# Modulated convolutions on one core: first product in three parts, H's products split over PE's row halves, adds moved to GpSimd, first edges stored apart

## The chip, the cores and the metric

The kernel runs on one core of one Trainium2 chip. The metric is the device time of one launch in microseconds. Engines are named as in the profile: PE (matmuls), PEld (its weight loads), DVE (VectorE), ACT (ScalarE), POOL (GpSimd), SP (SyncE, which issues most DMAs). Everything is fp32.

## What is computed

32 samples, 64 channels, 1024 positions, passed through four style-modulated convolutions with 3 taps and added to the input:

```
TYPES = ('same', 'upsample', 'same', 'downsample')
s = style @ mw.T + mb
weight = SCALE * w * s[:, None, :, None]
demod = rsqrt(sum(weight * weight, axis=(2, 3)) + EPS)
weight = weight * demod[:, :, None, None]
# same: conv(x, weight) + b;   upsample: transposed conv, stride 2, + b, then a [1,3,3,1] blur
# downsample: [1,3,3,1] blur, then conv with stride 2, + b
x = x + layer3(layer2(layer1(layer0(x))))
```

## The kernel before

Samples go in 16 pairs, one sample on partitions 0 to 63 and one on 64 to 127. Layers 1 to 3 are linear between the edges, so for each pair the kernel composes their weights into seven 64x64 matrices, called `H`, and applies these to layer 0's output. Three positions at each end of a row ("edges") follow the four layers one by one; all samples' edges are computed once, spread over the first three pairs.

All matmuls of the main loop use a 64x64 quarter of PE's array. A matmul's quarter is given by the half of the rows that its inputs are in (partitions 0 to 63 or 64 to 127: "row half") and the half of the output partitions. Each matmul is two records in the trace, and each of them has a weight load.

The order of work is written by hand, with one queue of instructions for each engine and semaphores between them. An iteration p of PE's loop is: `layer0_odd(p+1)` into `p_lo`, `layer0_even(p+1)` into `p_le`, `product_2(p)` into `p_m2`, `compose_R(p+2)` into `p_lo`, `product_1(p)` into one half of `p_m13`, `compose_H(p+2)` into `p_le`, `product_3(p)` into the other half of `p_m13`. The products multiply blocks of `Hw` (H with sums of its blocks) with `u` (layer 0's outputs at odd places, and differences of even and odd ones) or with `uu` (differences of differences, from which `product_2` gets 256 columns out of three products of 128 columns).

- ACT in iteration p: copies `p_lo` to `u` (L599), scales layer 0's weights, copies part of `product_2` to `t_sb` (L611), copies R to `R_sb` in two instructions (L593), scales `A_sb`, copies H to `Hw` (L605). `compose_H` waits for `R_sb`.
- DVE in iteration p: `make_diffs(p+1)` (L729), `add_parts(p)` (L758), `make_uu(p+1)` (L750), in the first pairs an edge step, `sum_taps(p+2)` (L736 adds the second half of H; L740, L742, L743 add blocks of `Hw`), `finish(p)` (L787), `add_x(p)` (L794).
- SP in iteration p: `place_H(p+2)` (L252, L253: copies `Hw` across the partition halves; `product_2(p+2)` waits for it), `load(p+4)`, `store(p)`. `store(p)` waits for POOL to have put the edges into `ot` (L235), and these are only known in iteration 2.
- POOL: edge preparations (`xse` L205, `z_st` L214, `prod` L222, `y_st` L226), then the edges of each pair into `ot`.

Ahead of the loop ("prologue") stand the styles, the demodulation on DVE, R and H of pairs 0 and 1, and three small constants (`yc`, `zc`, `oc`) that PE and DVE hand to each other: PE's L477 needs `yc`, its L484 needs `zc` and ACT's `o_st`.

## Time and profile before

| | us |
|---|---|
| median of 3 runs (lowest, highest) | 181.14 (180.51, 181.2) |
| the profiled execution's own time | 181.34 |
| its span, first to last instruction | 179.2 |
| PE busy / DVE busy / ACT busy / POOL busy | 170.8 / 125.4 / 57.2 / 15.4 |

The span is read from the trace; what the profiled execution's own time has beyond it (2.1 us) lies around the instructions. "Busy" counts an engine with at least one instruction under way, so four quarters at work count once.

### The profile page before, as it was taken

What the parts mean: (1) busy time and instruction counts of PE and PEld (TensorE: products, weight loads), DVE (VectorE), ACT (ScalarE), POOL (GpSimd) and SP (SyncE); (2) the same over time, 40 slices, a digit from 0 to 9 for tenths busy, and PEclk for the clock granted to TensorE, in tenths of its full rate; (3) what the DMA queues carried; (4) which work ended last, traced back from release to release, by engine and by line L of the source; (5) the groups of instructions that cost most, each with busy time, mean ns of one, the idle gap of its engine ahead of it and who ended that gap; (6) DMA issues with size and microseconds to landing.
All of it is one profiled execution on the core that took longest, in us unless ns stands there. A gap on an engine that the chain in (4) does not pass through costs nothing.

```text
span 179.2 us, 7986 instructions
## 1 busy us (share of the span) xinstructions
PE 170.8 (95%) x3567; PEld 155.4 (87%) x3567; DVE 125.4 (70%) x265; ACT 57.2 (32%) x126; POOL 15.4 (9%) x47
## 2 busy tenths in 40 slices
PE   7899999999999799999999999999999999999990
PEld 5598969986677498999999999999999999998960
DVE  7659755896776946758494949494949394958793
ACT  3433554122142233324151514243332424222110
POOL 7002202800001300200000000000000000000000
PEclk9958999999999999999999999999999999999999
DMA  4960003033000986827274645456463637333322
GB/s 135 365 75 2 4 0 91 4 89 123 0 5 4 273 278 240 225 88 222 98 170 161 159 166 152 177 115 214 103 224 91 237 89 236 93 121 75 140 117 117
DMA packets 11778, 23.65 MB, mean 132 GB/s; under 512 B 5184, under 2 KB 5728, under 8 KB 11744
## 3 DMA queue, kind: packets, MB, share of 16 engines
q1 hardware_dynamic: 11680, 23.12, 42.8%
q8 instruction: 28, 0.46, 1.1%
q14 instruction: 6, 0.05, 0.1%
q10 hardware_dynamic: 64, 0.02, 0.1%
HBM read 8.85 MB, written 8.39 MB: 96 GB/s over the span
## 4 chain that ended last, share of the span: by engine, by line
PE 91%; DVE 3%; issue 2%; ACT 1%; DVEq 0%
PE p_m L415 26%; PE p_le L354 14%; PE p_lo L354 13%; PE p_le L398 12%; PE p_m L433 11%; PE p_lo L385 5%; PE p_le L304 2%; PE p_m L294 1%; PE p_le L402 1%; PE p_m L512 1%; PE p_m L505 1%; DVE r_sb L769 1%; PE p_m L285 1%; PE p_m L343 1%; PE p_m L495 1%
## 5 line engine op out<-in xcount | busy, mean ns | idle before, releaser
L415 PE MATMUL p_m<-u,Hw 64*64 64x256 f32 x896 | 61.0, 377 | 0.3 <-DVE z_sb L787 0.3
L415 PEld LDWEIGHTS p_m<-u,Hw 64*64 64x64 f32 x896 | 46.9, 132 | 2.6 <-issue 0.5
L354 PE MATMUL p_lo<-xin,w0s 64*64 64x259 f32 x384 | 31.0, 406 | 0.0
L736 DVE SCALAR_TENSOR_TENSOR Hw<-p_le,pvec,Hw 128x320 f32<-128x320 f32 x16 | 8.8, 551 | 31.0 <-ACT Hw L605 31.0
L354 PE MATMUL p_le<-xin,w0s 64*64 64x260 f32 x384 | 30.1, 407 | 0.2 <-DVE Hw L743 0.2
L398 PE MATMUL p_le<-R_sb,F_st 64*64 64x192 f32 x320 | 30.0, 324 | 0.0
L398 PEld LDWEIGHTS p_le<-R_sb,F_st 64*64 64x64 f32 x320 | 25.8, 133 | 1.1 <-issue 0.4
L354 PEld LDWEIGHTS p_lo<-xin,w0s 64*64 64x64 f32 x384 | 21.8, 137 | 2.4 <-issue 0.3
L354 PEld LDWEIGHTS p_le<-xin,w0s 64*64 64x64 f32 x384 | 20.7, 137 | 3.4 <-issue 1.1
L605 ACT ACTIVATE Hw<-p_le,pvec 128x448 f32<-128x448 f32 x16 | 10.2, 635 | 37.0 <-PE p_le L398 37.0
L787 DVE SCALAR_TENSOR_TENSOR z_sb<-p_m,pvec,s_sb 128x512 f32<-128x512 f32 (+1 forms) x30 | 21.0, 742 | 0.9 <-PE p_m L415 0.9
L729 DVE TENSOR_TENSOR u<-p_le,u 128x1036 f32<-128x1036 f32 x16 | 19.7, 1231 | 1.7 <-PE p_le L354 1.7
L599 ACT ACTIVATE u<-p_lo 128x518 f32<-128x518 f32 x16 | 9.7, 604 | 34.2 <-PE p_lo L354 34.2
L433 PE MATMUL p_m<-uu,Hw 64*64 64x128 f32 x512 | 20.0, 269 | 0.0
L402 PE MATMUL p_le<-R_sb,F_st 64*64 64x128 f32 x256 | 19.6, 278 | 0.0
L611 ACT ACTIVATE t_sb<-p_m,pvec 128x256 f32<-128x256 f32 x16 | 9.0, 565 | 32.9 <-PE p_m L433 32.9
L758 DVE SCALAR_TENSOR_TENSOR s_sb<-p_m,pvec,t_sb 128x256 f32<-128x256 f32 x32 | 14.1, 486 | 6.6 <-ACT t_sb L611 6.5
L794 DVE TENSOR_TENSOR ot<-xin,z_sb 128x1018 f32<-128x1018 f32 x15 | 18.3, 1222 | 0.5
L433 PEld LDWEIGHTS p_m<-uu,Hw 64*64 64x64 f32 x512 | 17.6, 132 | 0.0
L402 PEld LDWEIGHTS p_le<-R_sb,F_st 64*64 64x64 f32 x256 | 17.0, 132 | 0.0
L433 PE MATMUL p_m<-u,Hw 64*64 64x128 f32 x256 | 13.6, 278 | 1.1 <-issue 1.1
L433 PEld LDWEIGHTS p_m<-u,Hw 64*64 64x64 f32 x256 | 12.4, 131 | 2.3 <-issue 1.6
(122 smaller groups left out, 155.9 us busy)
## 6 DMA issues: line engine op xcount, KB each, us to landing
...
bn<-in_L_cond_mod_b_dram ACTq DMA_DIRECT2D x1, 1.0 KB
```

What stands on the lines that cost most here:

```text
L354: ins = pe.matmul(bank[h * C:(h + 1) * C, s, 0:n], w0s[p % 2][rows, k, :], xin[p % NX][rows, i0:i0 + 2 * n - 1:2], start=(k == 0), stop=(k ...
L398: ins = pe.matmul(p_H[s * C:(s + 1) * C, c * C:(c + NR) * C], F_st[0:C, c, :], R_sb[s][0:C, 0:NR].rearrange("p a c -> p (a c)"), start=(c ...
L402: pe.matmul(p_Ho[s * C:(s + 1) * C, (c + 1) * C:(c + NR) * C], F_st[C:P, c, :], R_sb[s][C:P, 0:NR - 1].rearrange("p a c -> p (a c)"), star ...
L415: ins = pe.matmul(bank(h)[s * C:(s + 1) * C], tap(p, h, s, blk), u[p % 2][h * C:(h + 1) * C, s, j, k:k + NM], start=(k == 0), stop=(k == l ...
L433: ins = pe.matmul(p_m2[s * C:(s + 1) * C, h, c * NQ:(c + 1) * NQ], tap(p, h, s, blk), moving(s, slice(h * C, (h + 1) * C), k), start=(k == 0),
L599: act.activation(u[p % 2][:, :, 1, 0:NO], p_lo[:, :, 0:NO], ACT.Copy).then_inc(uo_made, 1)
L605: act.activation(Hw[p % NW][:, 0, 0:NH], p_H[:, 0:NH * C].rearrange("p (a c) -> p a c", c=C), ACT.Copy, scale=pcol(W_A0, p)).then_inc(H_ev ...
L611: act.activation(t_sb[p % 2][:], p_m2[:, :, 0:NQ], ACT.Identity, scale=pcol(W_D3, p), bias=pcol(W_C, p))\
L729: dve.tensor_tensor(u[p % 2][:, :, 0:3:2, 0:NO], even, u[p % 2][:, :, 1, 0:NO].unsqueeze(2).to_broadcast([P, 2, 2, NO]), ALU.subtract)\
L758: dve.scalar_tensor_tensor(out=s_sb[p % 2][:, h].rearrange("p (j b) -> p b j", b=2), in0=p_m2[:, h, NQ:3 * NQ].rearrange("p (b j) -> p b j ...
L787: dve.scalar_tensor_tensor(out=to[:, n0 + 2 * m0:n0 + 2 * NM].rearrange("p (m a) -> p a m", a=2), in0=p_m13[:, h, :, m0:NM], scalar=pcol(W ...
L794: dve.tensor_tensor(ot[p % NO_T][:, EDGE:L - EDGE], xin[p % NX][:, EDGE + 1:L - EDGE + 1], z_sb[p % 2][:, EDGE:L - EDGE], ALU.add).then_in ...
```

## The change

`product_1` made 16 matmuls of 256 columns. It now makes 16 of 128 columns from `uu`, and 8 more of 128 columns, `product_1_mid`, into free columns 256 to 383 of `p_lo`, after `compose_H`. `make_uu` therefore makes twice as much, in two instructions, and DVE adds the middle part with `s_sb` into `e_sb` (`add_mid`, two instructions) before `sum_taps`. `finish` is four instructions of 254 or 256 columns in place of two of 506 or 512. `layer0_odd(p)` has a new wait, for `e_made` of pair p-2. `compose_H` had 10 matmuls of 192 columns on the first row half and 8 of 128 on the second; it has 6 of 128 and 4 of 192 on the first, and 8 of 128 and 6 of 64 on the second, for which POOL copies three blocks of `F_st` to the other half once (`F_dup`). `add_x` and the sums of blocks of `Hw` (`sum_blocks`, with one more instruction, for blocks 12 and 13) go from DVE to POOL, apart from those of pair 0 and a part of the last `add_x`. PE no longer waits for the sums of blocks, only for `H_added`. POOL's preparations come in another order, from the moment `e2` is made. Pairs 0 to 3 are stored without their edges as soon as `add_x` is done, and their edges later, in pairs 4 to 7, by two small DMAs each.

```diff
+        def sum_blocks(eng, p):
+            eng.wait_ge(H_added, p + 1)
+            w = Hw[p % NW]
+            eng.tensor_tensor(w[:, 0, 9:6:-1], w[:, 0, 2:7:2], w[:, 0, 1:6:2], ALU.add).then_inc(H_sums1, 1)
+            eng.tensor_tensor(w[:, 0, 12:14], w[:, 0, 6:1:-4], w[:, 0, 4::-4], ALU.add).then_inc(H_sums, 1)
+            eng.wait_ge(H_sums1, p + 1)
+            eng.tensor_tensor(w[:, 0, 10], w[:, 0, 7], w[:, 0, 8], ALU.add).then_inc(H_sums, 1)
+            eng.tensor_tensor(w[:, 0, 11], w[:, 0, 9], w[:, 0, 0], ALU.add).then_inc(H_sums, 1)
...
+            pool.wait_ge(made["e2"], 1)
...
+            pool.wait_ge(copied["F_st"], 1)
+            pool.tensor_copy(F_st[C:P, NF:], F_st[0:C, 0:3]).then_inc(made["F_dup"], 1)
...
+            def add_x(p, n0, n1):
+                pool.wait_ge(z_made, 4 * (p + 1))
+                wait(pool, stored[p % NO_T], 16 * (p // NO_T))
+                pool.tensor_tensor(ot[p % NO_T][:, n0:n1], xin[p % NX][:, n0 + 1:n1 + 1],
+                                   z_sb[p % 2][:, n0:n1], ALU.add).then_inc(out_made, 1)
...
+            sum_blocks(pool, 1)
+            for p in range(PAIRS):
+                if p > 0:
+                    add_x(p - 1, EDGE, L - EDGE)
+                if p + 2 < PAIRS:
+                    sum_blocks(pool, p + 2)
+                if p >= LATE:
+                    put_edges(p)
+            add_x(PAIRS - 1, EDGE, NX_L)
...
-                sp.wait_ge(edge_put, p + 1)
...
+                if p < LATE:
+                    sp.dma_start(rows[:, EDGE:L - EDGE], ot[p % NO_T][:, EDGE:L - EDGE]).then_inc(stored[p % NO_T], 16)
+                else:
+                    sp.wait_ge(edge_put, p - LATE + 1)
+                    sp.dma_start(rows, ot[p % NO_T][:]).then_inc(stored[p % NO_T], 16)
...
+                wait(pe, e_made, 2 * (p - 1))
                 layer0(p, p_lo, NO, 1, lo_done)
...
-                wait(pe, H_sums, 2 * min(p + 1, PAIRS))
+                wait(pe, H_added, min(p + 1, PAIRS))
                 layer0(p, p_le, NE, 0, le_done)
...
                 for c in range(NF):
                     for s in range(2):
...
+                        part(p_H, 0, s, c, 0, 2 if c < 3 else 3, c, start=(c == 0), stop=(c == NF - 1))
                         if c < NF - 1:
...
+                            part(p_Ho, 1, s, c, 0, 2, c + 1, start=(c == 0), stop=False)
+                if p == 0:
+                    pe.wait_ge(made["F_dup"], 1)
+                for c in range(3):
+                    for s in range(2):
+                        ins = part(p_Ho, 1, s, NF + c, 2, 1, c + 2, start=False, stop=(c == 2))
...
             def product_1(p):
...
+                wait(pe, z_made, 4 * p)
+                ww = uu[p % 2]
+                part(p, lambda h: p_m13[:, h, 0, 0:NQ], (6, 2), lambda rows, s, k: ww[rows, s, 0, 0, k:k + NQ])
+                part(p, lambda h: p_m13[:, h, 0, NQ:2 * NQ], (4, 0), lambda rows, s, k: ww[rows, s, 0, 1, k:k + NQ])\
+                    .then_inc(m1_done, 1)
...
-                product(p, lambda h: p_m13[:, h, 0, 0:NM], 0, (6, 4, 2, 0))
...
+                part(p, lambda h: p_lo[:, h, 2 * NQ:3 * NQ], (12, 13),
+                     lambda rows, s, k: w[rows, s, 0, 2 * k + 1:2 * k + 2 * NQ:2]).then_inc(mid_done, 1)
...
                     compose_H(p + 2)
+                product_1_mid(p)
                 product_3(p)
...
+            def add_mid(p):
+                dve.wait_ge(mid_done, p + 1)
+                dve.wait_ge(s_made, 2 * (p + 1))
...
-                dve.tensor_tensor(ot[p % NO_T][:, EDGE:L - EDGE], xin[p % NX][:, EDGE + 1:L - EDGE + 1],
-                                  z_sb[p % 2][:, EDGE:L - EDGE], ALU.add).then_inc(out_made, 1)
+                dve.tensor_tensor(ot[p % NO_T][:, NX_L:L - EDGE], xin[p % NX][:, NX_L + 1:L - EDGE + 1],
+                                  z_sb[p % 2][:, NX_L:L - EDGE], ALU.add).then_inc(last_made, 1)
...
+                add_mid(p)
                 if p + 2 < PAIRS:
                     sum_taps(p + 2)
                 finish(p)
```

On PE, from `product_1(3)` to the next pair's layer 0, the kernel before has:

```order
L415 MATMUL p_m<-u,Hw 64x256 x16
L398 MATMUL p_le<-R_sb,F_st 64x192
L402 MATMUL p_le<-R_sb,F_st 64x128
...
L398 MATMUL p_le<-R_sb,F_st 64x192
L402 MATMUL p_le<-R_sb,F_st 64x128
L398 MATMUL p_le<-R_sb,F_st 64x192 x2
L415 MATMUL p_m<-u,Hw 64x256 x12
L354 MATMUL p_lo<-xin,w0s 64x259 x12
```

The changed kernel has in the same place (its L484 is the helper of all products of 128 columns, L449 that of `compose_H`):

```order
L484 MATMUL p_m<-uu,Hw 64x128 x16
L449 MATMUL p_le<-R_sb,F_st 64x128 x12
L449 MATMUL p_le<-R_sb,F_st 64x192
L449 MATMUL p_le<-R_sb,F_st 64x128
L449 MATMUL p_le<-R_sb,F_st 64x192
L449 MATMUL p_le<-R_sb,F_st 64x128
L449 MATMUL p_le<-R_sb,F_st 64x192 x2
L449 MATMUL p_le<-R_sb,F_st 64x64 x6
L484 MATMUL p_lo<-u,Hw 64x128 x8
L474 MATMUL p_m<-u,Hw 64x256 x12
L404 MATMUL p_lo<-xin,w0s 64x259 x12
```

The first product is shorter and has a second piece behind `compose_H`, in `p_lo`, which the next `layer0_odd` writes again.

On DVE, iteration 3 of the loop before:

```order
L729 TENSOR_TENSOR u<-p_le,u 128x2x2x259
L758 SCALAR_TENSOR_TENSOR s_sb<-p_m,pvec,t_sb 128x2x128 x2
L750 TENSOR_TENSOR uu<-u 128x516
L736 SCALAR_TENSOR_TENSOR Hw<-p_le,pvec,Hw 128x320
L740 TENSOR_TENSOR Hw<-Hw 128x3x64
L742 TENSOR_TENSOR Hw<-Hw 128x64
L743 TENSOR_TENSOR Hw<-Hw 128x64
L787 SCALAR_TENSOR_TENSOR z_sb<-p_m,pvec,s_sb 128x2x256
L787 SCALAR_TENSOR_TENSOR z_sb<-p_m,pvec,s_sb 128x2x253
L794 TENSOR_TENSOR ot<-xin,z_sb 128x1018
```

And of the changed kernel (L806 is `make_diffs`, L832 `add_parts`, L824 `make_uu`, L843 `add_mid`, L813 `sum_taps`, L856 `finish`):

```order
L806 TENSOR_TENSOR u<-p_le,u 128x2x2x259
L832 SCALAR_TENSOR_TENSOR s_sb<-p_m,pvec,t_sb 128x256 x2
L824 TENSOR_TENSOR uu<-u 128x516 x2
L843 SCALAR_TENSOR_TENSOR e_sb<-p_lo,pvec,s_sb 128x256 x2
L813 SCALAR_TENSOR_TENSOR Hw<-p_le,pvec,Hw 128x320
L856 SCALAR_TENSOR_TENSOR z_sb<-p_m,pvec,e_sb 128x2x127
L856 SCALAR_TENSOR_TENSOR z_sb<-p_m,pvec,e_sb 128x2x128
L856 SCALAR_TENSOR_TENSOR z_sb<-p_m,pvec,s_sb 128x2x127
L856 SCALAR_TENSOR_TENSOR z_sb<-p_m,pvec,s_sb 128x2x128
```

Three additions of `Hw`'s blocks and `add_x` are gone from the queue; a second `make_uu` and two instructions of `add_mid` stand ahead of `sum_taps`.

On POOL, the preparations for the edges in the kernel before:

```order
L205 TENSOR_TENSOR xse<-xe,style 64x256 x2
L214 COPY z_st<-w2T 64x64 x6
L222 TENSOR_TENSOR prod<-wn,coef 64x256 x3
L226 TENSOR_TENSOR y_st<-y_st,prod 64x256 x3
L228 COPY y_st<-y_st 64x128
```

And in the changed kernel, up to its loop:

```order
L228 TENSOR_TENSOR prod<-wn,coef 64x256 x3
L232 TENSOR_TENSOR y_st<-y_st,prod 64x256 x3
L234 COPY y_st<-y_st 64x128
L237 COPY F_st<-F_st 64x192
L243 COPY z_st<-w2T 64x64 x6
L248 TENSOR_TENSOR xse<-xe,style 64x256 x2
L196 TENSOR_TENSOR Hw<-Hw 128x3x64
L197 TENSOR_TENSOR Hw<-Hw 128x128
L199 TENSOR_TENSOR Hw<-Hw 128x64
```

The six additions for `y_st` move from the loop (where they waited for `t_made`) to the front, and `xse` behind `z_st`.

## Rows read from the trace of the kernel before

**Rows 1.** The page, busy time of each engine.
```profile
PE 170.8 (95%) x3567; PEld 155.4 (87%) x3567; DVE 125.4 (70%) x265; ACT 57.2 (32%) x126; POOL 15.4 (9%) x47
```

**Rows 2.** The page, the chain that ended last, shares by engine.
```profile
PE 91%; DVE 3%; issue 2%; ACT 1%; DVEq 0%
```

**Rows 3.** Timeline of PE, one iteration: start us, length us, what.
```profile
90.25 0.28 PE L433 MATMUL p_m<-u,Hw 64*64 64x128 f32 x2
...
91.64 0.32 PE L385 MATMUL p_lo<-A_sb,V_st 64*64 64x128 f32 x1
...
92.27 0.38 PE L415 MATMUL p_m<-u,Hw 64*64 64x256 f32 x1
...
94.00 0.27 PE L402 MATMUL p_le<-R_sb,F_st 64*64 64x128 f32 x1
...
96.70 0.39 PE L354 MATMUL p_lo<-xin,w0s 64*64 64x259 f32 x1
...
99.56 0.28 PE L433 MATMUL p_m<-u,Hw 64*64 64x128 f32 x2
```

**Rows 4.** Timeline of PE and SP, first pairs.
```profile
27.84 0.68 PE L433 MATMUL p_m<-u,Hw 64*64 64x128 f32 x16
...
62.48 0.69 PE L433 MATMUL p_m<-u,Hw 64*64 64x128 f32 x16 [1.11 <-issue]
...
57.86 0.35 SPq L261 DMA_DIRECT2D out_dram<-ot  x1
58.30 0.54 SPq L252 DMA_DIRECT2D Hw<-Hw  x1
```

**Rows 5.** Timeline of ACT, the iteration of rows 3.
```profile
92.07 0.57 ACT L611 ACTIVATE t_sb<-p_m,pvec 128x256 f32<-128x256 f32 x1 [1.77 <-PE p_m L433]
92.64 0.73 ACT L593 ACTIVATE R_sb<-p_lo,vec 128x192 f32<-128x192 f32 x2
```

**Rows 6.** Timeline of DVE, the iteration of rows 3.
```profile
92.67 0.88 DVE L758 SCALAR_TENSOR_TENSOR s_sb<-p_m,pvec,t_sb 128x256 f32<-128x256 f32 x2 [0.30 <-ACT t_sb L611]
93.46 0.69 DVE L750 TENSOR_TENSOR uu<-u 128x516 f32<-128x516 f32 x1
96.62 0.55 DVE L736 SCALAR_TENSOR_TENSOR Hw<-p_le,pvec,Hw 128x320 f32<-128x320 f32 x1 [2.47 <-ACT Hw L605]
```

**Rows 7.** Timeline of POOL, its preparations.
```profile
13.66 1.21 POOL L205 TENSOR_TENSOR xse<-xe,style 64x256 f32<-64x256 f32 x2 [9.75 <-DMA xe<-in_x_dram]
...
30.15 2.46 POOL L222 TENSOR_TENSOR prod<-wn,coef 64x256 f32<-64x256 f32 x3 [10.01 <-ACT t_sb L611]
```

**Rows 8.** Timeline of DVE beside those of POOL.
```profile
11.92 0.37 DVE L679 TENSOR_TENSOR pvec<-style,dm 64x16 f32<-64x16 f32 x2
...
13.79 1.11 DVE L679 TENSOR_TENSOR pvec<-dm 64x16 f32<-64x16 f32 x2
...
17.16 0.34 DVE L805 RECIPROCAL dr<-dq 128x32 f32<-128x32 f32 x1
...
19.68 0.22 DVE L688 SCALAR_TENSOR_TENSOR yc<-vec,yc 128x32 f32<-128x32 f32 x1
...
30.10 0.88 DVE L758 SCALAR_TENSOR_TENSOR s_sb<-p_m,pvec,t_sb 128x256 f32<-128x256 f32 x2 [0.70 <-ACT t_sb L611]
30.89 1.16 DVE L750 TENSOR_TENSOR uu<-u 128x516 f32<-128x516 f32 x1
```

**Rows 9.** Timeline of PE, end of the prologue.
```profile
21.60 0.85 PE L477 MATMUL p_m<-yc,z_st 128*128 128x32 f32 x6
24.64 1.61 PE L354 MATMUL p_lo<-xin,w0s 64*64 64x259 f32 x24
```

**Rows 10.** Timeline of PE and DVE, the last two pairs.
```profile
164.90 0.62 PE L433 MATMUL p_m<-u,Hw 64*64 64x128 f32 x11
...
171.25 3.25 PE L415 MATMUL p_m<-u,Hw 64*64 64x256 f32 x56 [0.26 <-DVE z_sb L787]
...
174.68 1.40 DVE L787 SCALAR_TENSOR_TENSOR ot<-p_m,pvec,r_sb 128x512 f32<-128x512 f32 x2 [0.20 <-PE p_m L415]
```

More of the change, by code:

```diff
@@ L168, in modulated_conv_kernel @@
         s_made = sem("s_made")
-        r_made = sem("r_made")
+        e_made = sem("e_made")
         z_made = sem("z_made")
@@ L418, in product, with part @@
                 return ins
+            def part(p, bank, blocks, moving):
+                for k, blk in enumerate(blocks):
+                    for s in range(2):
+                        for h in range(2):
+                            ins = pe.matmul(bank(h)[s * C:(s + 1) * C], tap(p, h, s, blk),
+                                            moving(slice(h * C, (h + 1) * C), s, k), start=(k == 0),
+                                            stop=(k == len(blocks) - 1), skip_group_check=True)
+                return ins
             def product_2(p):
@@ L773, in finish @@
-            def finish(p):
+                    dve.scalar_tensor_tensor(out=e_sb[:, h].rearrange("p (b j) -> p b j", b=2),
+                                             in0=p_lo[:, h, 2 * NQ:3 * NQ].unsqueeze(1).to_broadcast([P, 2, NQ]),
+                                             scalar=pcol(W_D3, p),
+                                             in1=s_sb[p % 2][:, h].rearrange("p (b j) -> p b j", b=2),
+                                             op0=ALU.mult, op1=ALU.add).then_inc(e_made, 1)
@@ new lines, in finish, with parity @@
+            def finish(p):
+                def parity(a, from_, add):
+                    for h in range(2):
+                        n0, n = EDGE + h * BASE, BASE // 4 if h == 0 else NQ
+                        to = z_sb[p % 2][:, n0:n0 + 4 * n].rearrange("p (j b a) -> p b j a", b=2, a=2)
+                        dve.scalar_tensor_tensor(out=to[:, :, :, a], in0=from_(h)[:, :, 0:n], scalar=pcol(W_D3, p),
+                                                 in1=add[:, h].rearrange("p (b j) -> p b j", b=2)[:, :, 0:n],
+                                                 op0=ALU.mult, op1=ALU.add).then_inc(z_made, 1)
@@ L791, in add_x @@
-            def add_x(p):
-                dve.wait_ge(z_made, 2 * (p + 1))
+                    dve.wait_ge(m1_done, p + 1)
+                else:
+                    dve.wait_ge(m13_done, p + 1)
+                dve.wait_ge(e_made, 2 * (p + 1))
+                wait(dve, out_made, p - 1)
+                parity(0, lambda h: p_m13[:, h, 0].rearrange("p (b j) -> p b j", b=2), e_sb)
+                if last:
+                    dve.wait_ge(m13_done, p + 1)
+                odd = p_le[:, :, 0:NM] if last else p_m13[:, :, 1]
```

177 lines of the change are left out of this document (85 added, 92 removed).

## Prediction

> **What bounds the kernel now.** I read the page first: PE is busy for 170.8 of 179.2 us, DVE for 125.4 [rows 1]. Then the chain that ended last, 91% of it on PE [rows 2]. So DVE's and POOL's work counts only where PE waits for it, and I read one iteration on PE's timeline [rows 3]. It starts at 90.25 and the next at 99.56, 9.31 us. By first records: `product_2` 1.39 (to 91.64), `compose_R` 0.63, `product_1` 1.73 (to 94.00), `compose_H` and `product_3` together 2.70 (to 96.70), both halves of layer 0 2.86. Between pair 3's start (62.48) and pair 14's (164.90) lie eleven such, 102.4 us [rows 4, 10].
>
> How many columns does that stand for? `product_1` is four groups of four quarters, 256 columns each: 1.73/4 = 0.43 us a group, so 0.00169 us for a column in each quarter. `product_2` is six groups of 128: 0.232 each, against 0.216 for half of 0.43. So PE is bound by the columns of the fuller row half, and small groups cost some 0.015 us extra. In `compose_H` each quarter of the first row half has 5 x 192 = 960 columns, 1.62 us at that price, the second row half 4 x 128 = 512. With `product_3`'s three groups (1.30) the first row half would need 2.92; the 0.2 short of that comes back in layer 0, whose 1557 columns (3 x 519) beside it would need 2.63 and take 2.86. I therefore cost these stages as one.
>
> **The change on PE, per pair.** `product_1`'s 16 matmuls of 128 are four groups like `product_2`'s: 4 x 0.232 = 0.93. The middle part is two more, 0.46. Together 1.39 for 1.73: **-0.34**. `compose_H` falls from 960 to 3 x 128 + 2 x 192 = 768 columns on the first row half; the second gets 512 + 3 x 64 = 704, its short ones beside the last 192. By columns that is -0.32. The twelve records of 64 columns have no row of their own inside `compose_H`, so I bound them: nothing, or up to 0.15 us, since `compose_R`, which has 64s too, takes 0.63 for 320 columns (0.54 by price). I take 0.1: **-0.22**. Sum -0.56, to 8.75.
>
> **The wait that appears.** `compose_H` waits for `R_sb`. In the iteration of [rows 3] ACT made `t_sb` at 92.07 to 92.64 and both R at 92.64 to 93.37 [rows 5], 3.12 us after the iteration's start, while PE came at 94.00, so it had 0.6 to spare. ACT's row does not move: it hangs on `product_2`'s end. PE now comes 0.80 sooner, at 1.39 + 0.63 + 0.93 = 2.95, and waits until some 3.2: **+0.25**. Queued behind it on PE are the middle part, `product_3` and layer 0. Period 8.75 + 0.25 = **9.0**, -0.31 a pair, over eleven pairs **-3.4**.
>
> **DVE in that period.** `add_parts` ends at 3.2 (92.67 + 0.88) [rows 6]. Then `make_uu` twice: two of 0.69, overlapping a little, 1.3, to 4.5. The middle part ends on PE at 3.2 + 1.4 + 0.46 = 5.05, plus its last record's 0.27: 5.3. `add_mid` has two instructions of `add_parts`' size, 0.88, and ends at 6.3. `layer0_odd` now waits for it and would come after `product_3`, at 5.05 + 1.3 = 6.35. That is even, and I take 0. If `add_mid` is 0.1 later, each pair pays 0.1. Behind `add_mid` stand `sum_taps` (0.55, to 6.9) and `finish`, four instructions of 0.49 or less overlapping, to 8.6; the next `product_1` needs them at 9.0 + 2.0. DVE's sum is about 6.6 of 9.0: covered.
>
> **POOL.** `add_x` has 1018 elements. The nearest rows are two-input additions of 256 in 0.62 (1.21 for two) and 0.82 (2.46 for three, beside DVE's work) [rows 7]; four times that is 2.4 to 3.3. It starts at the end of `finish`, 0.4 before the next iteration, and ends at 2.0 to 2.9, before `make_uu` at 3.2. Then `sum_blocks`, about 1.5, from 6.9 to 8.4. Nothing waits: `Hw` is placed for two iterations later. The Trainium skill (GPSIMD Engine Reference, Performance versus the Vector engine) has 4497 ns for 2048 elements against DVE's 2293 and advises against such moves. An estimate from it is 2.2 us for `add_x`, near the rows; it would speak against the change only if POOL were on PE's path.
>
> **Prologue.** What POOL does to DVE stands in [rows 8]. Two tiny additions took 0.37 together at 11.92, but 1.11 at 13.79, beside `xse`: each ended with a POOL instruction. `make_uu` took 1.16 beside `prod` in place of 0.69. `add_parts`, with one input in PSUM, kept its 0.88. So a DVE instruction with two SBUF inputs waits for POOL's. The change starts `prod` when `e2` is made, at about 12.3: six instructions like `prod`'s three (2.46 [rows 7]), 4.9 us, to some 17. In it lie five such DVE instructions ahead of `make_diffs(0)`. Each may wait some 0.45: +2.2, less the 0.75 that `xse` costs there now, +1.4. A second `make_uu` adds 0.6, and `xse`, now beside the next demodulation (17.16 to 19.90 today), up to 0.7: `yc` comes at 22.6 instead of 19.90. PE would be ready for it at 21.60 - 0.3 (shorter H) and waits until 22.65. Behind come DVE's `sum_blocks(0)` with an extra instruction of 0.3, ACT's copy across, `o_st`; layer 0 of pair 1, at 24.64 now [rows 9], starts near 26.4. PE no longer waits there for the sums, -0.35. Sum **+1.4**, bounds -0.5 (POOL costs nothing) and +1.8. The rule of the Trainium skill (SBUF — State Buffer, "two separate sides") is the same: the shared ports are an exclusive lock for a whole instruction. The rows agree.
>
> **First pairs.** From 27.84 to 62.48 PE has 34.6 us. The 1.11 before pair 3 had no releaser by the trace; SP shows it: `place_H(3)` (58.30) stood behind `store(0)` (57.86), which waited for the edges [rows 4]. Stores of pairs 0 to 3 no longer do: **-1.1**. In these three iterations DVE's edge steps stand between `make_uu` and `add_mid`, so `layer0_odd` waits and the 0.3 a pair is mostly lost; I keep -0.5 in all. Bounds -2.5 and -0.8. The eight small DMAs lie beside idle queues: 0.
>
> **The end.** Today pair 14's start (164.90) is 9.8 before `finish(15)` (174.68) and 11.2 before its end [rows 10]. New: PE reaches `product_1(15)` 4.08 + 1.39 = 5.5 after, but `finish(14)` runs behind `add_parts`, two `make_uu` and `add_mid`: 3.2 + 1.3 + 0.9 + 1.7 = 7.1. PE waits 1.7 (today 0.26). Then 0.93 + 0.46 + 1.3 + 0.25: PE ends at 10.1. Second half of `finish` 0.9 after 10.6, to 11.55. Then the last add in two pieces, 634 elements on DVE (about 0.8) and 384 on POOL (about 0.9): 0.9 together, 1.7 if one holds up the other. That is 12.5 to 13.3 for 11.2: +1.3 to +2.1. Both have two SBUF inputs, so I take **+2.0**.
>
> **Sum.** +1.4 - 1.1 - 0.5 - 3.4 + 2.0 = -1.6, to a span of 177.6. The profiled execution, 181.34, would become 179.7. It is 0.2 above the runs' median of 181.14. Forecast **179.6**.
>
> **Rivals.**
> - *DVE isn't held up in the prologue*, its instructions slip between POOL's: -0.5 in place of +1.4 there, **177.7**; the end's two pieces side by side as well, 176.9. For it: POOL's six additions wait for one another and leave gaps. Against: [rows 8], twice. 0.2.
> - *`compose_H` doesn't wait*, because ACT has R ready 0.25 sooner: 11 x 0.25 = 2.7 less, 176.9. Nothing in ACT's queue moved. 0.05.
> - *Slower: `add_mid` stops `layer0_odd` in every pair.* Place: PE's wait for `e_made`. It has 0.05 us to spare. If DVE starts 0.1 later after PE than I think (0.20 before L787 [rows 10]) and reads the part of `p_lo`, broadcast, at 512-column speed (two in 1.1 to 1.4), the period is 9.3 and all of the steady gain is gone: -1.6 + 3.4 = +1.8, **183.0**. It decides against the change from about 0.15 a pair with the prologue as above. 0.15.
> - *The gains are real but the ends eat them*: prologue +1.8, first pairs -0.8, end +2.2, steady -3.0: 181.4, no change. 0.15.
> - The forecast itself, 178.3 to 180.6: 0.45.
>
> **Range and chances.** A difference of 0.5% (0.9 us) is about what a measurement of this kernel can tell. From the cases: faster than 180.2 0.61, slower than 182.0 0.18. The range reaches from the first rival to short of the slower one: 176.8 to 182.5.
>
> **What would show it.** PE's timeline of a middle pair: start to start 9.0, with about 0.25 idle before L449, 0 before L404. If L404 waits for L843, the slower rival holds. `product_1` 0.93. L477 near 22.6 and the two tiny additions before `make_diffs(0)` stretched. No wait before pair 3. L484 of pair 15 waiting about 1.7 for L856. The forecast is wrong if the period is under 8.8 or over 9.2, or if layer 0 of pair 1 starts before 25.

## The result and the profile after

The changed kernel takes **183.61 us** (median of 20 runs, 181.35 to 184.8), the kernel before 181.14 (median of 20, 180.42 to 182.52): ratio 1.0099 [1.0072, 1.0126], slower by 1%. The forecast was 179.6, faster. The profiled execution took 182.9 us with a span of 181.1, so it is 0.7 shorter than the median, and what is read from it is that much smaller. Here and below a time is the median of all executions, and a ratio, with its 95% interval, leaves out executions in the slow state, those more than 1.5% above the fastest of their kernel.

The page, busy time of each engine, the answer to [rows 1]:

```profile
PE 163.4 (90%) x4015; PEld 140.3 (77%) x4015; DVE 134.0 (74%) x285; ACT 57.0 (31%) x126; POOL 73.5 (41%) x120
```

PE is busy for 7.4 us less while the span is 1.9 us longer, so PE stands still somewhere. PE's timeline for a middle pair, the answer to [rows 3] (here a row is a whole group of matmuls):

```profile
128.03 0.66 PE L484 MATMUL p_m<-u,Hw 64*64 64x128 f32 x16
...
129.37 0.75 PE L436 MATMUL p_lo<-A_sb,V_st 64*64 64x128 f32 x24
129.93 1.07 PE L484 MATMUL p_m<-uu,Hw 64*64 64x128 f32 x32
131.18 1.53 PE L449 MATMUL p_le<-R_sb,F_st 64*64 64x128 f32 x48 [0.18 <-issue]
132.46 0.71 PE L484 MATMUL p_lo<-u,Hw 64*64 64x128 f32 x16
132.92 1.54 PE L474 MATMUL p_m<-u,Hw 64*64 64x256 f32 x24
134.26 1.60 PE L404 MATMUL p_lo<-xin,w0s 64*64 64x259 f32 x24
...
137.03 0.67 PE L484 MATMUL p_m<-u,Hw 64*64 64x128 f32 x16
```

128.03 to 137.03 is 9.00 us, the period of the forecast, with its small wait ahead of L449 (`compose_H`, for `R_sb`) and none at L404. The loss is in pairs that don't look like this. Call the time from one start of `layer0_odd` to the next an interval. From pair 4 to pair 15 there are eleven; they are 9.0 to 9.1 us, but for two: 11.13 (77.04 to 88.17) and 9.96 (97.18 to 107.14). PE's timeline in these two, and the weight loads at the first:

```profile
78.43 1.07 PE L404 MATMUL p_le<-xin,w0s 64*64 64x260 f32 x10
80.92 0.91 PE L404 MATMUL p_le<-xin,w0s 64*64 64x260 f32 x11 [1.42 <-issue]
...
103.11 1.20 PE L449 MATMUL p_le<-R_sb,F_st 64*64 64x128 f32 x32 [0.18 <-issue]
105.00 0.54 PE L449 MATMUL p_le<-R_sb,F_st 64*64 64x192 f32 x14 [0.68 <-issue]
...
80.93 0.42 PEld L404 LDWEIGHTS p_le<-xin,w0s 64*64 64x64 f32 x10 [1.90 <-issue]
```

PE stops in the middle of a group whose inputs it is already using, and the trace names no releaser. Such a stop is called a hole below. For its place, an iteration p is counted from the start of `product_2(p)`: the first hole is in iteration 4, in `layer0_even(6)`, the second in iteration 7, in `compose_H(9)`. The intervals lose more (2.1 and 0.95) than PE's idle shows (1.42 and 0.68), since the ends of matmuls are modelled.

Last, the two ends of the kernel: PE's timeline, the answer to [rows 9, 10], and DVE's and POOL's last rows:

```profile
22.35 0.83 PE L553 MATMUL p_m<-yc,z_st 128*128 128x32 f32 x6 [0.71 <-issue]
25.40 0.54 PE L560 MATMUL p_m<-zc,o_st 128*64 128x32 f32 x12 [0.77 <-ACT o_st L719]
25.88 1.61 PE L404 MATMUL p_lo<-xin,w0s 64*64 64x259 f32 x24
...
164.16 0.67 PE L484 MATMUL p_m<-u,Hw 64*64 64x128 f32 x16
...
171.52 1.11 PE L484 MATMUL p_m<-uu,Hw 64*64 64x128 f32 x32 [1.83 <-DVE z_sb L856]
...
176.27 0.82 DVE L877 TENSOR_TENSOR ot<-xin,z_sb 128x634 f32<-128x634 f32 x1
...
176.32 1.63 POOL L255 TENSOR_TENSOR ot<-xin,z_sb 128x384 f32<-128x384 f32 x1 [2.28 <-DVE z_sb L856]
```

By the forecast's own parts (`product_2` of pairs 0, 3 and 14 starts at 28.69, 61.81 and 164.16 in the changed kernel):

| part | before | forecast | after | off by |
|---|---|---|---|---|
| to pair 0 | 27.84 | 29.24 | 28.69 | -0.55 |
| pairs 0 to 3 | 34.64 | 33.04 | 33.12 | +0.1 |
| pairs 3 to 14 | 102.42 | 99.0 | 102.35 | +3.3 |
| pair 14 to the end | 14.3 | 16.3 | 16.9 | +0.6 |
| span | 179.2 | 177.6 | 181.1 | +3.5 |

### The profile page after: what moved, and what is told of

Read it like the earlier page. It is cut to its first block and busy times, and to the rows that moved or that the text cites. A ratio compares the mean times of both kernels' runs of the same rounds, so it can differ in the third digit from the quotient of the medians.

```text
span 181.1 us, 9008 instructions
## 1 busy us (share of the span) xinstructions
PE 163.4 (90%) x4015; PEld 140.3 (77%) x4015; DVE 134.0 (74%) x285; ACT 57.0 (31%) x126; POOL 73.5 (41%) x120
## 5 line engine op out<-in xcount | busy, mean ns | idle before, releaser
L255 POOL TENSOR_TENSOR ot<-xin,z_sb 128x1018 f32<-128x1018 f32 (+1 forms) x16 | 37.2, 2324 | 13.6 <-DVE z_sb L856 13.6
L484 PE MATMUL p_m<-uu,Hw 64*64 64x128 f32 x1024 | 35.3, 269 | 1.8 <-DVE z_sb L856 1.8
L484 PEld LDWEIGHTS p_m<-uu,Hw 64*64 64x64 f32 x1024 | 30.8, 132 | 2.1 <-DVE z_sb L856 2.1
L404 PE MATMUL p_le<-xin,w0s 64*64 64x260 f32 x384 | 27.5, 404 | 1.4 <-issue 1.4
L806 DVE TENSOR_TENSOR u<-p_le,u 128x1036 f32<-128x1036 f32 x16 | 19.8, 1235 | 11.9 <-PE p_le L404 11.9
L449 PE MATMUL p_le<-R_sb,F_st 64*64 64x128 f32 (+2 forms) x768 | 25.1, 269 | 2.7 <-issue 2.5
L404 PE MATMUL p_lo<-xin,w0s 64*64 64x259 f32 x384 | 27.2, 409 | 0.1
L449 PEld LDWEIGHTS p_le<-R_sb,F_st 64*64 64x64 f32 x768 | 21.6, 133 | 5.9 <-issue 5.7
L404 PEld LDWEIGHTS p_le<-xin,w0s 64*64 64x64 f32 x384 | 18.9, 137 | 6.5 <-issue 1.9
L843 DVE SCALAR_TENSOR_TENSOR e_sb<-p_lo,pvec,s_sb 128x256 f32<-128x256 f32 x32 | 14.0, 479 | 12.4 <-PE p_lo L484 12.4
L474 PE MATMUL p_m<-u,Hw 64*64 64x256 f32 x360 | 23.1, 375 | 0.0
L832 DVE SCALAR_TENSOR_TENSOR s_sb<-p_m,pvec,t_sb 128x256 f32<-128x256 f32 x32 | 14.0, 479 | 11.0 <-ACT t_sb L688 11.0
L404 PEld LDWEIGHTS p_lo<-xin,w0s 64*64 64x64 f32 x384 | 16.5, 137 | 6.7 <-issue 3.5
L824 DVE TENSOR_TENSOR uu<-u 128x516 f32<-128x516 f32 x32 | 20.7, 689 | 0.1
L856 DVE SCALAR_TENSOR_TENSOR z_sb<-p_m,pvec,e_sb 128x254 f32<-128x254 f32 (+1 forms) x32 | 18.7, 665 | 0.2
L474 PEld LDWEIGHTS p_m<-u,Hw 64*64 64x64 f32 x360 | 17.4, 132 | 0.5
L856 DVE SCALAR_TENSOR_TENSOR z_sb<-p_m,pvec,s_sb 128x254 f32<-128x254 f32 (+1 forms) x30 | 17.1, 652 | 0.0
```

Of the source, the lines that this page charges most:

```text
L255: pool.tensor_tensor(ot[p % NO_T][:, n0:n1], xin[p % NX][:, n0 + 1:n1 + 1], z_sb[p % 2][:, n0:n1], ALU.add).then_inc(out_made, 1)
L404: ins = pe.matmul(bank[h * C:(h + 1) * C, s, 0:n], w0s[p % 2][rows, k, :], xin[p % NX][rows, i0:i0 + 2 * n - 1:2], start=(k == 0), stop=(k ...
L449: return pe.matmul(bank[s * C:(s + 1) * C, to * C:(to + n) * C], F_st[rows, f, :], R_sb[s][rows, a:a + n].rearrange("p a c -> p (a c)"), s ...
L474: ins = pe.matmul(bank(h)[s * C:(s + 1) * C], tap(p, h, s, blk), u[p % 2][h * C:(h + 1) * C, s, j, k:k + NM], start=(k == 0), stop=(k == l ...
L484: ins = pe.matmul(bank(h)[s * C:(s + 1) * C], tap(p, h, s, blk), moving(slice(h * C, (h + 1) * C), s, k), start=(k == 0), stop=(k == len(b ...
L806: dve.tensor_tensor(u[p % 2][:, :, 0:3:2, 0:NO], even, u[p % 2][:, :, 1, 0:NO].unsqueeze(2).to_broadcast([P, 2, 2, NO]), ALU.subtract)\
```

## What the holes are

The page's list of DMA queues has one of kind "instruction", with 28 packets before and 32 after:

```profile
q8 instruction: 32, 0.52, 1.2%
```

0.52 MB in 32 packets is 16 KB each. Each f32 matmul is four instructions of PE, two loads and two passes (`compose_H`'s 24 matmuls show as x48, with x48 loads). Counted so, PE's program has 7,289 instructions before (1,787 matmuls and 141 others, nearly all waits) and 8,185 after (2,011 and 141), 28.5 and 32.0 times 256. So a packet is taken to be a block of 256 of them. A steady iteration has 432 instructions before and 488 after: a block lasts 9.31 x 256/432 = 5.5 us before and 9.0 x 256/488 = **4.7 us** after, on average. With the program numbered from 0, the holes stand at instruction 3280 = 13 x 256 - 48 and 4560 = 18 x 256 - 48. Places of the form 256k - 48 are called edges. Why 48 short of the full block no run shows, and the number depends on the count (the prologue's seven transposes, counted as four instructions each, show one load and one pass); that all holes share it does not.

The DMA view of the changed kernel has no packet of this queue from 74.0 to 78.4, where the load and the store of a pair fill the engines, and one behind them. The whole list of queues for 74 to 78.4, then for 78.4 to 79.5:

```profile
q1 hardware_dynamic: 280, 1.02, 74.4%
...
q8 instruction: 1, 0.02, 5.4%
q1 hardware_dynamic: 2, 0.00, 1.0%
```

5.4% of 16 engines over 1.1 us is 0.95 us, which ends at some 79.5, and PE goes on at 80.92. Where the DMA engines are little used, the packet mostly starts 0.4 to 1.5 us behind PE's passing of the edge before. Here that edge (12 x 256 - 48) was passed at 73.4. **Theory F**: PE has one block ahead and no more. The next is asked for at an edge; its transfer queues behind load and store; it must be there at the next edge, 4.7 us later on average. By these rows it needs some 0.8 to be asked for, 0.95 to move and 1.4 to be used. As an estimate, that leaves some 1.5 us for a queue, and load and store with H's transfers make up to 4.

The profiles of all the kernels below bear this out. Each has one packet for each edge of PE's program (28 before, 32 after, 35 in run 2, 30 in run 6). PE never passed an edge sooner than 1.2 us after the end of the packet that was asked for at the edge before. At the 37 edges where its weight loads stood still for more than 0.25 us, it went on 1.2 to 1.6 us after that end. In the kernel before, the closest case is 1.9 us: there the packets come in time.

The Trainium skill (Runtime: NRT & Kernel Launch, Instruction fetch mechanics) has the blocks of 16 KiB as 256 instructions, with which the counts agree, and calls the cost of crossing one "mostly hidden". Here it is 2.1 us for one crossing: the measurement decides. It also gives PE a store of 2048 instructions. The holes at one edge end behind the packet asked for at the edge before, so no run here shows more than one block ahead.

## Experiments

Each comparison is with the kernel before, run on the same chip.

**1. Stores cut short** (the changed kernel).

```
+                elif p < PAIRS - 1:
+                    sp.wait_ge(edge_put, p - LATE + 1)
+                    sp.dma_start(rows[:, 0:64], ot[p % NO_T][:, 0:64]).then_inc(...)
```

> The changed kernel with the stores of pairs 4 to 14 cut to their first 64 columns (the rest of those rows isn't written). Nothing that PE waits for changes. Theory F (PE's own instructions arrive late: they come by DMA in 16 KB blocks, and the block's transfer waits behind loads and stores): the two holes inside a stage, 1.42 and 0.68 us in the changed kernel's profile, are gone, every middle pair takes 9.0 us, the span falls by about 3 us to 178.0, the time to about 180. Theory D (the holes are a wait for data or for a buffer): holes and span stay, 181 us. What stays under both: prologue +0.85 and end +2.6 against the kernel before.

The kernel leaves most of these rows of the output unwritten. 181.89 us, 1.0047 [1.0019, 1.0075], where 180 was expected. The second hole went and every interval from 88 us on is 9.0 to 9.1. The first stayed, 1.41 at 80.81. It follows the store of pair 3, which this run left whole. So the next run cuts that too.

> Every store of pairs 0 to 14 writes the first 64 columns only (for pairs 0 to 3 columns EDGE to 64); the rest of those rows of the output is left unwritten, the last pair's is whole. In the run with only the stores of pairs 4 to 14 cut, TensorE's hole of 1.41 us at 80.8 stayed and the later one went. Theory F (TensorE waits for its own code, whose transfer stands behind the load and the store): with store 3 short too, the hole at 80.8 goes or falls under 0.3 us, all intervals of layer0_odd from pair 5 on are 9.0 to 9.1, span 178.2 to 178.8. Rival A (an engine's result is late there and the stores have nothing to do with it): the hole stays at 1.4 us, span 180.0. Rival B (the load alone holds the code up): the hole shrinks to 0.7 to 1.2 us, span 179.3 to 179.8.

180.89 us, 0.9943 [0.9903, 0.9982]. All eleven intervals from pair 4 to 15 are 8.99 to 9.03; no hole. The span, 179.3, missed the expected range, because this execution's first `layer0_odd` came at 10.64 (9.89 in the changed kernel's) and the prologue was 1.6 longer by pair 1 (27.44 for 25.88). Without that it is 177.7. Rivals A and B fall: the hole needs the store. That leaves open whether it needs its bytes or its place in the queue; run 10 tells.

**2. The kernel before with more instructions**: `product_1` and `product_3` in halves of 128 columns, 28 matmuls more for a pair, the same columns.

```
+                for q in (0, NQ):
                     for k, blk in enumerate(blocks):
```

> The kernel before with products 1 and 3 in halves of 128 columns: the same columns, data and DMAs, but 28 more matmuls a pair, each four instructions. Theory F: an instruction block of 256 lasts 4.5 us of work in place of 5.5, less than in the changed kernel (4.7), so holes without a releaser appear in the middle of stages, 3 us or more in all; with 0.2 us a pair for small groups (14 of 0.232 for 7 of 0.43) the span is 179.2 + 3.2 + 3 = 185.5 or more. Theory D: no such holes, only the small groups, 182.4.

191.08 us, 1.053 [1.0482, 1.0578]. An iteration has 544 instructions and its clean interval is 9.4, so a block lasts 4.4 us. The kernel that had no hole in its steady pairs now has four over 1 us, at 68.57, 119.71, 130.24 and 141.31, with intervals of 10.65 to 12.35, and 35 packets for 9,081 instructions. All four stand within one instruction of an edge. Nothing of the change is in it but the number of instructions.

**3. GpSimd's sums for `y_st` behind `sum_blocks(1)`** (the prologue's term).

```
             sum_blocks(pool, 1)
...
+            for k in range(K):
+                pool.tensor_tensor(prod[:, k], ...)
...
```

> The changed kernel with POOL's six additions for y_st moved from the moment e2 is made to behind sum_blocks of pair 1. If POOL's instructions hold up DVE's two-input ones in the prologue, the tiny additions before make_diffs(0) are back to about 0.2 us each, yc comes 1.5 us sooner and product_2(0) starts at 27.3 in place of 28.69; the first pairs may give 0.3 back, where make_uu(1) meets the additions. The time is 1 us lower than the changed kernel's if the holes stay as they are. If POOL does not matter, product_2(0) stays at 28.7.

182.08 us, 1.0044 [1.0016, 1.0073]. DVE's small instructions are short again (0.37 for the 0.92 that the changed kernel's `pvec` row shows at 14.72, below), but then `make_diffs(0)` waits for PE:

```profile
14.13 0.37 DVE L757 TENSOR_TENSOR pvec<-dm 64x16 f32<-64x16 f32 x2
15.80 1.24 DVE L807 TENSOR_TENSOR u<-p_le,u 128x1036 f32<-128x1036 f32 x1 [1.03 <-PE p_le L405]
```

So `product_2(0)` starts at 27.82, 0.9 sooner and not 1.4: layer 0 of pair 1 starts at 25.00 in place of 25.88, while the first interval grew by 0.36 (10.43 for 10.07). The holes stayed (1.15 at 80.11, 0.44 at 104.01).

**4. The load behind the store and behind `e_made`.**

```
+                store(p)
                 if p + 4 < PAIRS:
+                    sp.wait_ge(e_made, 2 * (p + 2))
                     load(p + 4)
-                store(p)
```

> The changed kernel with SP's queue in another order: store(p) first, and load(p+4) waits for e_made of pair p+1, about 4 us later, so that a load and a store no longer run together. Theory F: PE's instruction blocks wait behind one transfer of 0.5 MB (1.7 us) at most in place of two (4 us), the holes shrink to under 0.5 us in all, span 178.0 to 178.6. Theory D: no change, or worse if the load comes too late (it has 4 us to spare).

183.3 us, 1.0108 [1.0065, 1.015]: no gain. The two holes went and others came: 0.47 at 74.20, 0.97 at 137.26, 0.41 at 147.36. The largest stands at instruction 6352 = 25 x 256 - 48, an edge too; its packet came at 134.9, behind the load issued at 131.56. Where the DMA engines are busy decides which edge is hit.

**5. Useless waits to hold the edges in place.**

```
             def compose_H(p):
+                for _ in range(48 if p > 5 else 240 if p == 5 else 0):
+                    pe.wait_ge(ident_made, 1)
```

(two such waits make one instruction; 240 is 512 in the second run)

> Nothing of the computation changes. TensorE's program gets useless waits (on a semaphore that has long been set) ahead of compose_H: 96 + 24 instructions once, in iteration 3, and 24 in each iteration after it, so that an iteration from there on is 512 instructions, exactly two blocks of 256, and the edges of the blocks stand at one place of every iteration: 85 instructions behind the start of product_2 (1.2 us after it) and in product_1_mid (4.6 us). Theory F: the code's transfer is asked for some 0.8 us behind an edge, the first falls ahead of the load and the store, the second behind them but in time, so from pair 5 on TensorE has no hole over 0.3 us, however regular or not the intervals were before; each interval is 9.0 plus what 24 waits cost over the present wait there (0 to 0.6 us), all equal within 0.1. Rival A (the holes of 1.42 at 80.9 and 0.68 at 105.0 come from an engine that is late in those pairs): a hole of 0.5 to 1.5 us stays within one pair of either place.

> As the run with 96 + 24 waits in iteration 3, but 232 + 24 there, so that the two edges of blocks in each iteration stand 204 instructions behind the start of product_2 (2.9 us, at the end of product_1) and 460 behind it (7.5 us, in layer0_even), which is how they stood in the iteration of the hole at 80.9. The same number of instructions in each iteration as the other one. Theory F: the code asked for at 3.7 us waits behind the load and the store to 7.0 or later and TensorE stands 1 to 2 us at the start of layer0_even or behind it, in most iterations from 4 to 10, as long as there are loads: span 5 to 12 us over the other padded run beyond the 136 more waits (at most 4 us) in iteration 3. Rival A: no difference in the intervals of pairs 5 to 15 between the two padded runs.

218.03 us, 1.2048 [1.2006, 1.209], and 236.43, 1.3057 [1.2996, 1.3118]. Neither test decides anything, because of its own cost. An already satisfied wait of PE takes 0.115 us: 136 more instructions of waits in iteration 3 lengthen its interval from 22.93 to 38.59. PE's timeline in a middle iteration of the first:

```profile
111.59 1.07 PE L486 MATMUL p_m<-uu,Hw 64*64 64x128 f32 x32
114.63 1.53 PE L451 MATMUL p_le<-R_sb,F_st 64*64 64x128 f32 x48 [1.97 <-issue]
```

The 24 waits stop PE for 2 us in each iteration. Intervals from iteration 4 on are 10.8 to 11.0, every second or third one 12.4 to 13.0, in both runs, and no hole at `layer0_even` came in the second. A block then lasts 5.4 us or more, nearly the 5.5 of the kernel before, so theory F would have no hole either; the runs don't tell it from rival A. The long interval looked at, 117.71 to 130.09 of the first run, has a stretch at a granted clock of 0.50 behind the stop (busy of PE, PEld, DVE, ACT and POOL with counts, then granted clock, DMA share and GB/s):

```profile
128.00:130.00 2.00, 2.00 (x24) 1.92 (x20) 1.30 (x3) 0.00 (x0) 0.62 (x2) 0.50 0.00 0
```

**6. The old `compose_H` in the changed kernel** (22 lines back to the kernel before's).

```
-                        part(p_H, 0, s, c, 0, 2 if c < 3 else 3, c, ...)
+                        ins = pe.matmul(p_H[s * C:(s + 1) * C, c * C:(c + NR) * C], F_st[0:C, c, :], ...)
```

> The changed kernel with compose_H as it was: 22 matmuls with all of H's products in the order of before, the row halves uneven. The prediction's term was -0.22 us an iteration for the new compose_H, with R_sb's wait of 0.25 us beside it. With the old one compose_H takes 0.22 us more, and what it waits for R_sb is as before. So clean intervals of layer0_odd should be 9.22 to 9.25 if the term is right, and 9.0 if it is worth nothing. By theory F an iteration is then 480 instructions or less, not 488, and a block of code lasts 4.9 us: holes of TensorE move to other pairs or shrink, at 256k-48 instructions wherever they are; sum of holes over 0.3 us from 60 us on 0 to 2.5 us, median 182 to 185.

186.62 us, the median of four from 184.02 to 188.13; the ratio, 1.0207 [1.0147, 1.0268], rests on the two shorter ones, 184.02 and 185.82, whose mean is inside the expected range. The profile is of the longest, so its holes may be larger than usual. Its clean intervals are 9.33, above the expected range, so the new `compose_H` is worth 0.33 of them, not 0.22. Holes stand at instructions 2000, 4048 and, within two matmuls, 7120 (8, 16 and 28 x 256 - 48): 1.70 at 58.96, 0.96 at 102.30, 0.35 at 164.22. The old `compose_H` has 18 matmuls and not the 22 expected, so an iteration has 464 instructions and a block lasts 5.1 us; that did not save this order, since a hole comes where an edge meets busy DMA engines.

**7. PE's program shifted by 188 instructions.**

```
-            for _ in range(4):
-                pe.matmul(p_le[:, 1, 0:256], pe_warm[:, 0:P], pe_warm[:], start=True, stop=True)
+            for _ in range(51):
+                pe.matmul(p_le[0:C, 1, 0:8], pe_warm[0:C, 0:C], pe_warm[0:C, 0:8], start=True, stop=True)
```

> TensorE's four warm-up matmuls of 128x256 at the start (16 instructions, 3.8 us) are replaced by 51 small ones (204 instructions); nothing else changes, so every later instruction of TensorE stands 188 places further along its program, and the edges of the blocks of 256 move by 188 against the work. In the changed kernel the holes stood where an edge fell 204/460 and 276 instructions behind the start of a product_2, in iterations 4 and 7. Here such edges fall: 276 in iteration 4, 460 in iteration 12, where the DMA engines have no load left. Theory F: the hole of 1.4 us at layer0_even of iteration 4 is gone; one of 0.3 to 1.0 us stands in compose_H of iteration 4 or of 3; none from iteration 6 to 14; so the sum of late intervals falls from 3.1 to under 1.2 us and the median from 183.6 to 181.2 to 182.4. Rival A (a late engine): both holes stay in their pairs, median 183 to 184.5.

192.05 us, 1.0592 [1.0521, 1.0662]. The small matmuls took 11.05 us in place of 3.78, so the whole kernel starts 8.0 later; from there on the intervals are what was asked for. The hole of 1.42 at iteration 4's `layer0_even` is gone. Iteration 4 has a stop inside its `compose_H` instead, as expected, in the interval ahead (9.85), and those from pair 6 to 12 are 9.0 to 9.1. One part of the expectation is wrong. No hole was to come from iteration 6 to 14, since the edge in `layer0_even` of iteration 12 finds no load; that edge costs nothing indeed, but the one in `layer0_even(13)`, at the end of iteration 11, still meets the last load. It is the largest stop of all. PE's timeline, and the windows around it (columns as under run 5):

```profile
149.18 1.61 PE L404 MATMUL p_lo<-xin,w0s 64*64 64x259 f32 x24
152.78 2.71 PE L404 MATMUL p_le<-xin,w0s 64*64 64x260 f32 x24 [1.99 <-issue]
155.15 1.20 PE L484 MATMUL p_m<-u,Hw 64*64 64x128 f32 x16
...
151.00:153.00 2.00, 0.22 (x4) 0.20 (x7) 0.58 (x2) 0.79 (x2) 1.61 (x3) 1.00 0.41 82
153.00:155.00 2.00, 2.00 (x24) 1.72 (x20) 0.00 (x0) 0.00 (x0) 1.01 (x1) 0.51 0.53 155
```

Instruction 6864 = 27 x 256 - 48. The load and store ahead of it had been issued at 144.92 and 145.36, the packet came at 150.4. Behind the hole the granted clock was 0.51, the level of 1.2 GHz, and `layer0_even` took 2.71 for 1.59: the interval is 12.83, 3.8 over. So the same program with the same work has its largest hole seven iterations later when its instructions stand 188 further on. That is not a late engine.

**8. The ends.** Three edits: the order of run 3; `product_1` of the last pair into `p_lo`, waiting for `e_made`; the last add wholly on DVE. Alone, and with run 7's shift:

```
-                wait(pe, z_made, 4 * p)
+                last = p == PAIRS - 1
+                wait(pe, e_made if last else z_made, 2 * p if last else 4 * p)
...
-            add_x(PAIRS - 1, EDGE, NX_L)
```

> Three edits of the changed kernel at its ends: GpSimd's sums for y_st come behind sum_blocks(1), as in the run that gave 182.08 alone; product_1 of the last pair goes to p_lo and waits for e_made, not for the z_made of the pair before; VectorE does the whole last add. The forecast put the end at +2.0 and it was +2.6. If those 2.6 are product_1's wait of 1.83 us for z_sb and GpSimd's piece of 1.63 us, the two edits take 1.3 to 2.0 off (span from layer0_odd of pair 15 to the end 18.1 to 18.7 where it was 19.7) and with the order on GpSimd the median is 180.2 to 181.4. If the end is set by something else (VectorE's own chain), the end stays within 0.5 of 19.7 and the median at 181.6 to 182.6. Holes of TensorE stay at 256k-48 instructions.

> The three edits of the ends and the 51 small warm-up matmuls together. If the code's edges and the ends are separate costs, the gains add: holes from pair 5 on sum to under 1.2 us, end as in the run of the three edits, median 178.2 to 180.0, faster than before by 0.6 to 1.6%. If theory F is wrong, the median is that of the run of the three edits within 0.4.

The first: 180.62 us, 0.9944 [0.9911, 0.9978]. This is as expected: from `layer0_odd` of pair 15 to the end it takes 18.6 in place of 19.7. The wait of 1.83 for `z_sb` is gone and the last add is one row of DVE:

```profile
174.01 1.22 DVE L881 TENSOR_TENSOR ot<-xin,z_sb 128x1018 f32<-128x1018 f32 x1
```

The second, expected at 178.2 to 180.0: 188.64 us, 1.0431 [1.0371, 1.049]; as in run 7, the start pays 7.2 us, intervals lose 0.5 to 1.9 in three other places, and nothing is gained by shifting.

**9. The second evacuation of R by DVE.**

```
-                for s in range(2):
+                for s in range(2 if p < 2 else 1):
...
+                if p + 2 < PAIRS:
+                    evac_R1(p + 2)
```

> The second evacuation of R of each pair goes from ScalarE to VectorE, behind make_diffs, so that compose_H need not wait for it. The forecast put this wait at 0.25 us of each iteration. If it is so and nothing replaces it, clean intervals of layer0_odd fall from 9.00 to 8.75 to 8.85. If VectorE's longer queue delays the sums of z or the evacuation of H, they stay at 9.0 or rise. By theory F a block then lasts less than 4.6 us, the slack of the code's transfer is smaller and the holes of TensorE grow in number or size: late intervals sum to 3 to 6 us and the median is 182 to 185 in spite of the shorter clean interval.

181.64 us, 1.0001 [0.9971, 1.0032]. Clean intervals are 8.70 and `compose_H` has no wait, so the wait for `R_sb` was worth 0.30, not 0.25. Over eleven pairs that is 3.3 us, of which the times show 2.0 (183.61 to 181.64): the first three intervals grew by 0.8, and holes make intervals of 10.59, 9.95 and 9.35, together 3.8 over, where the changed kernel lost 3.1. A block lasts 4.6 us.

**10. The store later, nothing else.**

```
                 if p + 4 < PAIRS:
                     load(p + 4)
+                if p >= 3:
+                    sp.wait_ge(H_done, min(p + 4, PAIRS))
                 store(p)
```

> The changed kernel with one wait more: SyncE issues the store of a pair from 3 on behind compose_H of the running iteration, some 2 us later than now, so that the load (2 us of the DMA engines) and the store (2 us) no longer form one burst. All bytes are moved. Theory F: the code's transfer that stood behind both at 74.0 to 78.4 now gets in behind the load alone; TensorE's hole of 1.42 us at layer0_even of iteration 4 shrinks to 0 to 0.5 us, and the loss of that interval from 2.1 to under 1; the one in iteration 7 (asked for behind H's transfers, not the store) may stay; median 181.0 to 182.8. Rival B (the load alone holds the code up): the hole stays within 0.3 of 1.42, median 183 to 184. Rival C (the late store now stands ahead of H's placement, which is issued 6 us after the start of product_2, and product_2 waits): every interval grows by 0.3 to 1 us, median 186 or more.

**179.66 us, 0.9903 [0.988, 0.9925].** All bytes are moved, all instructions are there, and no hole is left: of the eleven intervals from pair 4 to 15 ten are 9.00 to 9.02 and the last 9.11. PE's timeline at the place of the first hole, SyncE's queue ahead of it, and the instruction queue for 75.3 to 76.7:

```profile
76.97 1.60 PE L406 MATMUL p_lo<-xin,w0s 64*64 64x259 f32 x24
78.36 1.59 PE L406 MATMUL p_le<-xin,w0s 64*64 64x260 f32 x24
...
72.89 0.33 SPq L283 DMA_DIRECT2D xin<-in_x_dram  x1
75.55 0.35 SPq L299 DMA_DIRECT2D out_dram<-ot  x1
...
q8 instruction: 1, 0.02, 4.5%
```

The load is issued at 72.89, the store only at 75.55, and the packet, at 75.6, goes in the gap between them: 3.0 us sooner than in the changed kernel. The gain was larger than expected (181.0 to 182.8), since the second hole went too: 3.9 us between the medians and 3.2 between the two profiled executions (182.9 and 179.7), where the two long intervals had lost 3.1.

**11. The same line in the kernel before.**

> The kernel before with the same late store (from pair 3 on the store waits for compose_H of the running iteration). Its steady intervals are 9.30 to 9.32 us with no hole, a block of code lasts 5.5 us there. Theory F: the late store gives back only what the changed kernel lost, so nothing is to be had here: intervals 9.30 to 9.32, median within 0.5 of 181.4. Rival D (the late store is an improvement of its own, whatever the code): median 179 to 180.5, as it took 3.9 us off the changed kernel. Rival C (it delays H's placement): intervals over 9.4, median over 182.

181.57 us, 0.9989 [0.9968, 1.001]: nothing. The line gives back what the change had lost and has no gain of its own.

**12. Together.**

> The three edits of the ends (180.62 alone) with the late store. If the late store takes the hole at layer0_even of iteration 4 (loss 1.58 in that run) and the rest stays, the median is 179.0 to 180.2; if it does nothing, 180.4 to 181.

> The three edits of the ends with VectorE doing the second evacuation of R. Clean intervals were 8.70 with it against 9.01, and eleven of them are 3.4 us; but first pairs grew by 0.5 to 0.8 us and the holes were as large as in the changed kernel. So the median should be 180.62 less 1.0 to 2.4: 178.2 to 179.6. If the shorter interval only makes larger holes, as the forecast's bare sum would not see, it stays above 180.

> All of it: ends, R by VectorE, late store. If the store's place is worth 0.5 to 1.6 us as theory F says, the median is that less than the run without it, 177.0 to 179.0; with a block of code lasting 4.5 us the slack is small, so one or two holes of 0.5 to 1 us remain.

Ends and late store 177.96, 0.981 [0.9789, 0.983]; ends and R by DVE 178.7, 0.9897 [0.9821, 0.9974]; all three **174.88**, 0.9643 [0.961, 0.9676]. The first and the last are under their expected ranges: the late store was to be worth 0.5 to 1.6 in the last and is worth 3.8. Without it intervals of 10.60, 10.17 and 9.40 stand among those of 8.70, with it only one, 9.07, with no hole. It is the fastest kernel of this study, 3.6% below the kernel before.

## Why the prediction was wrong

**The step that failed** is "Period 8.75 + 0.25 = 9.0, -0.31 a pair, over eleven pairs -3.4". The period is right to 0.01 us. What is wrong is to take it eleven times: pairs 3 to 14 gained 0.1 in place of 3.4. Of the 3.3 missing, 3.1 were lost in two intervals in which PE waited for its own program (runs 1, 2, 7, 10, 11); with the store later, all eleven came out at 9.0 to 9.1. The sum counted the columns of the new matmuls and never their instructions, which went from 432 to 488 an iteration, so it put a wait for them at nothing without a reason. The rival that came nearest to the time (183.0) had another mechanism, `add_mid` stopping `layer0_odd`, and that doesn't occur: a likeness of numbers. DVE's row of `add_mid` in the middle pair ends at 134.10, and L404 starts at 134.26 without a wait:

```profile
133.22 0.88 DVE L843 SCALAR_TENSOR_TENSOR e_sb<-p_lo,pvec,s_sb 128x256 f32<-128x256 f32 x2 [0.91 <-PE p_lo L484]
```

**`compose_H` and its wait**: -0.33 in place of -0.22 (run 6) and a wait of 0.30 in place of 0.25 (run 9). Together they would leave the period 0.06 shorter than forecast; by difference, `product_1` with its middle part gives -0.28 for -0.34, which makes that up.

**Prologue**: the mechanism held, +0.85 for +1.4. DVE's instructions beside POOL's `prod` and `y_st` are stretched, as the forecast had it:

```profile
13.42 0.60 DVE L765 SCALAR_TENSOR_TENSOR da<-da,dr 128x64 f32<-128x64 f32 x1
14.06 0.62 DVE L765 SCALAR_TENSOR_TENSOR dm<-da,dr 128x64 f32<-128x64 f32 x1
14.72 0.92 DVE L756 TENSOR_TENSOR pvec<-dm 64x16 f32<-64x16 f32 x2
15.67 0.60 DVE L760 TENSOR_SCALAR vec<-dm,biases 128x32 f32<-128x32 f32 x1
```

These five instructions took 1.06 us in run 3, where POOL is idle beside them, and 2.74 here: 1.7 more, where the forecast had 2.2. POOL's six instructions took 4.5 us for the 4.9 allowed and the rest of `yc`'s chain was less held up. The rival with no hold-up falls.

**First pairs**: 33.12 for 33.04; the wait of 1.11 before pair 3 is gone, as forecast.

**The end**: +2.6 for +2.0. The wait for `z_sb` is 1.83 for 1.7; the last add lies in a row as feared, 384 elements on POOL in 1.63 while DVE did 634 in 0.82, together 1.7. The rest is mostly in `finish`, whose halves were put at 0.9 and take 1.13 to 1.16, and whose second half waits for the first:

```profile
174.12 1.15 DVE L856 SCALAR_TENSOR_TENSOR z_sb<-p_m,pvec,e_sb 128x254 f32<-128x254 f32 x2
175.11 1.13 DVE L856 SCALAR_TENSOR_TENSOR z_sb<-p_le,pvec,s_sb 128x254 f32<-128x254 f32 x2
```

The last add so begins 12.1 us after pair 14's start, for the 11.55 of the sum.

With the late store (run 10) the time is 179.66, beside the forecast's 179.6. That is in part luck: prologue and end are off by -0.55 and +0.6, and `compose_H` and its wait by -0.11 and +0.05 in each pair.
